# Decoder layer on one core: alternating query tiles in attention, value products in bursts of two tiles, turning steps and norm constants moved

## What is computed

```python
h = layernorm(x)
q, k, v = split(h @ w_qkv.T + b_qkv)      # 32 query heads, 8 key/value heads of width 32
q, k = rope(q), rope(k)
s = q @ k.T / sqrt(32), causal             # four query heads share a key head
x = x + (softmax(s) @ v) @ w_o.T + b_o
x = x + fake_quant(layernorm(x)) @ fake_quant(ctx)            # "cross"
x = x + layernorm(x) @ W_org.T + sum_e c_e * (lora_e down, up) # "base", "down", "up"
```

## Time and profile before

| what | value |
|---|---|
| median of 3 runs | 717.89 us (717.77 to 718.95) |
| the profiled execution's own time | 717.73 us |
| its span, first to last instruction | 715.9 us |
| PE busy | 660.2 us, 92% of the span |
| DVE, ACT, POOL busy | 430.2, 424.7, 281.2 us |
| mean granted clock of PE | 0.976 |
| units of attention, first to last score | 77.8 to 486.4 us |

### The profile page before, as it was taken

One profiled execution on the slowest core, in us unless ns is written; L12 is line 12 of the kernel. 1 busy time (PEld: TensorE's weight loads), 2 busy tenths in 40 slices (PEclk: granted clock), 3 DMA queues, 4 the chain that ended last, 5 costly groups with the idle time before them and its releaser, 6 DMA issues.

```text
span 715.9 us, 12713 instructions
## 1 busy us (share of the span) xinstructions
PE 660.2 (92%) x4512; PEld 530.3 (74%) x4512; DVE 430.2 (60%) x1137; ACT 424.7 (59%) x1025; POOL 281.2 (39%) x301
## 2 busy tenths in 40 slices
PE   4996899999999899999989699999999698999998
PEld 3985677898777678777756577777878576788886
DVE  6796677875877634677676966442326788811122
ACT  5425678878787747599977675755315782611320
POOL 2046645534444354455320720506715024814520
PEclk9998999999999999999999899999999989999999
DMA  7646854752555733225561340505326352614102
GB/s 264 227 152 187 244 164 124 213 149 76 144 159 160 201 87 99 94 56 150 178 181 60 100 130 1 147 1 156 124 75 234 100 187 82 189 47 117 44 16 102
DMA packets 43934, 93.46 MB, mean 131 GB/s; under 512 B 5505, under 2 KB 5889, under 8 KB 42433
## 3 DMA queue, kind: packets, MB, share of 16 engines
q1 hardware_dynamic: 34416, 66.45, 29.3%
q0 software_dynamic: 3696, 15.73, 9.5%
q10 hardware_dynamic: 5760, 10.49, 4.0%
HBM read 72.72 MB, written 19.92 MB: 129 GB/s over the span
## 4 chain that ended last, share of the span: by engine, by line
PE 72%; DVE 12%; ACT 6%; issue 4%; POOL 4%; DMA 1%; ACTq 0%; DVEq 0%
PE dense L1040 47%; PE probt L932 8%; PE score L920 5%; PE pv L947 5%; POOL w_lo L1653 2%; DVE stats L1333 2%; ACT prob_all L1131 2%; DVE xres L1435 2%; PE score L1040 1%; DVE w_lo L1269 1%; PE misc L956 1%; PE probt L901 1%; ACT w_hi L1084 1%; PE misc L986 1%; PE misc L901 1%
## 5 line engine op out<-in xcount | busy, mean ns | idle before, releaser
L1040 PE MATMUL dense<-w_hi,act_t 128*128 128x512 f32 (+1 forms) x684 | 226.0, 391 | 5.4 <-POOL act_t L1664 1.8
L1289 DVE CUSTOM_DVE_ANT_0 prob_all<-score,mask_sb 128x128 f32<-128x128 f32 (+3 forms) x256 | 123.2, 488 | 121.0 <-PE score L920 119.1
L1653 POOL TENSOR_TENSOR w_lo<-stage,w_hi 128x512 fp32r<-128x512 f32 x85 | 110.1, 1303 | 201.8 <-ACT w_hi L1084 201.6
L1131 ACT ACTIVATE prob_all<-prob_all,neg_max 128x128 f32<-128x128 f32 (+3 forms) x256 | 142.7, 558 | 37.4 <-DVE neg_max L1289 36.0
L1040 PEld LDWEIGHTS dense<-w_hi,act_t 128*128 128x128 f32 x684 | 128.5, 193 | 28.4 <-issue 3.8
L1040 PE MATMUL dense<-act_t,w_hi 128*128 128x512 f32 x408 | 138.2, 420 | 3.3 <-DVE xres L1435 2.1
L1040 PE MATMUL dense<-w_lo,act_t 128*128 128x512 f32 (+1 forms) x372 | 135.5, 385 | 1.6 <-ACT w_lo L1089 1.4
L932 PE MATMUL probt<-ident_sb,prob_all 128*128 128x128 f32 x640 | 113.7, 277 | 5.1 <-ACT prob_all L1140 4.5
L1084 ACT ACTIVATE w_hi<-stage 128x512 fp32r<-128x512 f32 x117 | 72.0, 623 | 45.6 <-PE dense L1040 34.8
L1140 ACT ACTIVATE prob_all<-probt 128x128 f32<-128x128 f32 (+3 forms) x160 | 68.5, 428 | 47.8 <-PE probt L932 47.0
L932 PEld LDWEIGHTS probt<-ident_sb,prob_all 128*128 128x128 f32 x640 | 80.0, 142 | 22.0 <-issue 7.5
(11 more groups left out here) (168 smaller groups left out, 858.7 us busy)
## 6 DMA issues: line engine op xcount, KB each, us to landing
q_stack<-rope_dram POOLq DMA_DIRECT2D x15, 768.0 KB, 7.3
stage<-in_w_qk SPq DMA_DIRECT2D x40, 256.0 KB, 3.0
rope_dram<-act_t ACTq DMA_DIRECT2D x40, 256.0 KB, 2.5
stage<-in_w_o SPq DMA_DIRECT2D x32, 256.0 KB, 2.9
stage<-in_ctx_kv SPq DMA_DIRECT2D x24, 256.0 KB, 3.4
stage<-in_w_org SPq DMA_DIRECT2D x24, 256.0 KB, 3.1
xres<-in_x SPq DMA_DIRECT2D x8, 512.0 KB, 7.0
prob_all<-in_x SPq DMA_DIRECT2D x8, 512.0 KB, 5.9
```

The costliest lines, as they stand in the source:

```text
L1040: last = engine.matmul(dst, lhs, rhs, start=(k == 0 and c == 0), stop=(k == g.kts - 1 and c == len(pairs) - 1))
L1131: engine.activation(prob[:, u % P_SLOTS, 0:length], prob[:, u % P_SLOTS, 0:length], ACT.Exp, bias=neg_max[:, m:m + 1], scale=-1.0, accum_o ...
L1289: engine.tensor_tensor_reduce(prob[:, u % P_SLOTS, 0:length], score_bank[u % 2][:, 0:length], mask_sb[:, S - length:S], -1.0, HIGHEST, ALU ...
L1653: engine.tensor_tensor(slot_lo(p, 0, NW), raw_of(p), slot_hi(p, 0, NW).bitcast(F32), ALU.subtract).then_inc(g_piece, 1)
```

## The change

1. `unit(u)`: a group's 16 units come in two runs of eight. The first alternates tile 0 and tile 3, head by head; the second alternates tile 1 and tile 2.
2. `values`: the value products of eight units (two tiles) come in one burst, at the same lag of 5 slots behind the last of them. There are two bursts for a group, not four; the products are the same.
3. `prob_t` becomes a ring of 6 couples of 5 blocks (1 + 4 or 2 + 3), so 12 units. Small arrays move into `bias_v` and `ln_i` into `ln_s` to make room. `probt_on` is adapted: DVE gets units 0 and 3 of four, later 0 and 3 of eight.
4. The turning of the second sequence's tiles moves three slots later (slots 28 + 4t and 30 + 4t); applying the norm stays where it is.
5. The first two steps of that norm chain are done column by column, so eight instructions on one column each and not two on four.
6. `constants` moves from slot 10 to slot 5 in DVE's program.

```diff
+PROBT_COUPLES = 6
+BURST = 8
+TILE_ORDER = (0, 3), (1, 2)
...
-                at = HEAD + 17 + 4 * t + 2 * half
+                at = HEAD + 20 + 4 * t + 2 * half
...
-        probt_on = ["vector" if u % (2 if u < UNITS // 2 else 4) == 1 else "scalar" for u in range(UNITS)]
+        probt_on = ["vector" if u % (4 if u < UNITS // 2 else 8) in (0, 3) else "scalar" for u in range(UNITS)]
...
-            return u // (NT * GROUP), u // GROUP % NT, u % GROUP
+            gi, place = divmod(u, NT * GROUP)
+            return gi, TILE_ORDER[place // BURST][place % 2], place % BURST // 2
+
+        def turned_to(u, a, b):
+
+            start = u // 2 % PROBT_COUPLES * 5 * P + (u % 2) * (unit(u - 1)[1] + 1) * P
+            return prob_t[:, start + a:start + b]
...
-                if i == 0 and gi:
+                for u in range(w * BURST, (w + 1) * BURST):
+                    e.wait_ge(*probt_done(u))
+                if w * BURST % (NT * GROUP) == 0 and gi:
                     e.wait_ge(v_attn, gi)
...
+                for side in range(2):
+                    i = unit(w * BURST + side)[1]
+                    e.wait_ge(*evacuated("v", b, 0, i))
...
-                if 0 <= u - PV_LAG < UNITS and (u - PV_LAG) % GROUP == GROUP - 1:
-                    values((u - PV_LAG) // GROUP)
+                if 0 <= u - PV_LAG < UNITS and (u - PV_LAG) % BURST == BURST - 1:
+                    values((u - PV_LAG) // BURST)
...
-                if u >= PROBT_SLOTS:
-                    e.wait_ge(t_pv, (u - PROBT_SLOTS) // GROUP + 1)
+                if u >= 2 * PROBT_COUPLES:
+                    e.wait_ge(t_pv, (u - 2 * PROBT_COUPLES) // BURST + 1)
...
-                ln(engine.tensor_scalar(w, var, EPS, -ROOT_SCALE, ALU.add, ALU.mult))
+                for t in range(NT):
+                    ln(engine.tensor_scalar(w[:, t:t + 1], var[:, t:t + 1], EPS, -ROOT_SCALE, ALU.add, ALU.mult))
...
+                if j == HEAD - 3:
                     constants()
```

60 lines of the change are left out of this document (28 added, 32 removed).

## The result

The changed kernel takes **722.42 us** (median of 5 runs, 720.96 to 723.37) against 717.89 (716.67 to 718.95) for the kernel before on the same chip: a ratio of 1.005, 95% interval 1.0034 to 1.0066. It is 4.5 us slower. (Of all runs behind this document one was slow, at 754.5 us, of small_alt; it stands in that kernel's median of ten, but not in its ratio.) The prediction was 706.6 us, with a range of 701.5 to 712.2; the time is outside it and on the other side of no change.

The account below looks back on a forecast made before the run. PE was taken to bound mid-attention; from 335 to 420 us, the PE/DVE/ACT loop and side work. Gains 6.4 + 0.3 + 1.9 + 2.65 = 11.25 us off 717.73, plus 0.16, gave 706.6 us, range 701.5 to 712.2.

Parts of the forecast that it names:

- Bursts, 6.4 us: Value products on PE: 32 fewer bursts, 27 counted on the path at 0.236 us each, gain 6.4 us.
- gap for each tile: Rival: two tiles in a burst pay the gap twice, so the burst part does nothing; 713.0 us, chance 0.06.
- Later waits, 0.3 us: PE in attention: a group's first burst comes four slots later, so its wait for L1310 goes, gain 0.3 us.
- Alternation, +1.9 us: Attention loop: alternating long and short units saves part of PE's waits for L920 and L932; 1.9 us, bounds -2 and 9.
- Head, 2.65 us: Before the first score: later turnings fill PE's idle time, with norm chain and constants; 3.05 + 0.2 - 0.6 us.
- The term for the constants, -0.6: DVE in the head: constants in slot 5 delay a rotation; loss of 0.6 us, bounds -0.6 and 1.0.
- the chain on DVE: Norm chain of the second sequence: one-column steps beside POOL save 0.2 us, bounds 0 and 1.9.
- In the clock I count nothing: Head: no gain counted for the granted clock, though less idling may spare a fall, put at 1.5 us.
- Slower: Rival: new PE waits in attention where long maximum and copy meet side work, 2.7 us each; some 720, chance 0.07.
- Given back: Rival: only the bursts gain, loop waits stay and units begin no earlier; 711.5 us, chance 0.2.

Follow-up runs that it names:

- small_alt: The change without edits 4 to 6, three once-per-group jobs on ACT and DVE cut to 128 of 512 columns from the second group on: 717.88 us, ratio 0.999.
- bursts_only: The kernel before with two bursts of two tiles per group, old order of units and old head: 717.29 us, ratio 0.998.
- mixed: The kernel before with two bursts per group, edits 4 to 6, and rotated tiles' high-half stores issued by SP, old order: 712.15 us; again 712.44.
- attn_only: The change without its head part, so edits 1 to 3 alone: 721.09 us, ratio 1.0055.
- high_later: The change without edits 4 to 6, with ACT's copy of the attention output and POOL's part behind it one slot later: 724.14 us, ratio 1.0066.
- long_first: The change without edits 4 to 6, each pair swapped, tile 3 before 0 and 2 before 1: 718.63 us, ratio 0.9997.
- head_only: The kernel before with only edits 4 to 6, on the ring layout of bursts_only: 715.44 us, ratio 0.997.

## Why the prediction was wrong

**What bounds the kernel.** "There PE sets the pace, and work taken off PE shortens the run by as much." The first half of this is right, the second was the error behind two of the terms. A PE that is busy 118.91 of 120 us shows no slack on PE; it says nothing on how close the others are behind it. DVE and ACT are busy three quarters of the time on the mean, but in several groups there is a place where their queues are full enough for PE to meet them. bursts_only edits PE's products alone, and it gains 1.2 us; the same with short jobs on ACT and DVE gains 4.4, and with full jobs and the stores issued by SP 3.0 to 3.3.

**Bursts, 6.4 us.** The price of a burst was right to the hundredth (0.23 to 0.24 us), and so was that it isn't paid between tiles. The rule of the Trainium skill, "TensorEngine Tiling (Array Packing)", section "Key Properties", that a change of tiling mode drains TensorE, agrees: 40 products in two tiles show one gap. As a gain it is 6.6 under the alternation, 1.2 alone and 3.0 to 3.3 in the mixed kernel. The term was well sized for the kernel in which it was made, where ACT's and DVE's jobs stand elsewhere, and too large for the old order. The rival "gap for each tile" is refuted.

**Later waits, 0.3 us.** The wait for L1310 is gone from the list, as forecast.

**Alternation, +1.9 us.** This is the step that failed. In place of a gain of 1.9 it measured -9.2 alone and -3.8 with the bursts (attn_only against bursts_only), the new split of the copies included, outside the bounds of -2 to 9. I asked what the waits of the kernel before would do and took half of them as gain. I didn't ask what stood beside the units in the slots that change: which jobs come once for a group, at which lag, and how long the unit beside them is before and after. The earlier trace rows has a wait of 0.3 us for L1310 and nothing for L1140 (0.4 us in the trace, which the sum left out), and I read that as a loop with room. Its room lay at least in part in the short units, and the edit moved these: that is shown for the waits in the tenth slot (shorter jobs, a copy moved or the pairs swapped take 1.6, 2.4 and 2.9 us off units 16 to 128 in small_alt, high_later and long_first). For what stays with every help, 5.6 to 6.1 us, no cause is shown; it stays open.

**Head, 2.65 us.** Alone it gave 3.0, near the sum, but by luck. The term for the constants, -0.6, had the wrong sign. The rotation behind slot 5 did come 0.7 us later (DVE's L1435 at 43.95, now L1448 at 44.65), but the 2.4 us that the five instructions took in slot 10 went as well, and the norm chain began 1.8 us earlier (53.81 for 55.57), outside the bound of 1.0. PE's wait for the norm fell from 4.88 to 2.5 us, and a new wait of 3.1 us came at 69.5, for DVE's copy of a turned half (L1395). The first score came 3.7 to 3.9 us earlier, the chain on DVE saved 0.36 us from its first instruction to the end of its last (0.2 expected), and its shape was as forecast. The eight one-column instructions ran beside a POOL instruction, and the steps with two inputs behind them took the wait:

```profile
53.81 0.32 DVE L1367 TENSOR_SCALAR ln_s<-mean_var 128x1 f32<-128x1 f32 x4
54.17 0.33 DVE L1370 TENSOR_SCALAR ln_s<-ln_s 128x1 int32<-128x1 int32 x4
54.53 0.52 DVE L1372 TENSOR_TENSOR ln_s<-ln_s 128x4 f32<-128x4 f32 x1
...
55.09 1.22 DVE L1374 TENSOR_TENSOR ln_s<-ln_s 128x4 f32<-128x4 f32 x1
```

But its gain is carried by little: in head_only 1.0 us of it reaches group 1 and the rest is clock. In the whole change nothing is left: group 0 takes 3.4 to 3.7 us back, against 2.6 in head_only and 1.3 in mixed, whose clock didn't fall there. "In the clock I count nothing" was the wrong choice where an edit moves idle time.

**The rivals.** "Slower" had the right mechanism (a long maximum and a long copy meet side work on DVE or ACT) and the right price to start with, and it was given 7%. It was wrong in place and number: I looked for it from 335 to 420 us and at units 0 to 5, and asked for five places; it came most clearly at the same slot of groups 3, 4 and 5. Its argument against, that "the mean work in a slot is the same", is the same mean over stages that misled the first part. "Given back" was right on the bursts alone.

## What to carry over

Before units are reordered, list for each slot what else stands in the queues of the engines that serve it, at its fixed lag, and how long the unit beside it is before and after: the short units may be there to cover it. A saving on the busiest engine is worth only as much as the next engine has room in its fullest slots, and the cheapest test of that is the saving alone, and the saving with the neighbours' jobs cut short. Where moving one job by a slot gives 2.4 us in one stretch and costs as much in the next, as here, compare starts of the same unit by stretch and not totals.

## What the runs showed of the hardware

- A burst of 32-column products costs PE 0.09 us on entry and 0.14 at its end beyond the products, with 8, 32 or 40 of them in one or two tiles.
- The second of two DMA issues in a row on ACT took 0.46 us in the kernel before and 0.45 to 2.1 us in kernels with another order of units, other bursts or shorter jobs; ACT's next instruction waits. In 33 of the 36 cases over 0.6 us, counted from 88 to 340 us in all kernels that issue these stores on ACT, no other engine had issued a DMA for over 3 us, so what it waits for isn't in the rows. The Trainium skill, "Perfetto Trace Analysis", section "DMA Instruction — HWDGE (DVE, Sync)", says that the profiled time of such an issue holds a wait for the descriptor generator, which it calls shared by the DVE and Sync sequencers; the issues here are ACT's, of which that section doesn't speak, and no run here shows which part of the time grew.
- The granted clock's fall moved with PE's idle time: before it lay in the 23 us ahead of the first score (0.85), afterwards behind it (0.56 from 80 to 86 us), with full clock ahead. But idle time alone doesn't settle it: head_only and mixed wait alike for units 3 and 4 (1.5 and 1.4 us), and from 80 to 86 us the first had 0.72 and the second 1.00; and mixed run again had 0.80 from 360 to 385 us where it had had 0.93. And 1.6 us of head_only's gain were a fall at unit 137 that didn't come, though PE idled there as long as before.
